# Which rows of the matrix form a block: blocks of neighbouring rows, or every 20th row (19th in the second half)

## The reference

```
a1 = adj * (y @ y.T);  a1 = a1 / max(rowsum(a1), 1e-12)
x  = layernorm(x + 0.9 * (a1 @ x) + 0.1 * h0)
f  = tanh(x @ W_proj + b_proj) @ W_gcn
x  = layernorm(x + relu(tanh(adj * adj) * (adj > 0) @ f + b_gcn))     # top 350 of a row; no row has more
```

## Time and profile before

| | |
|---|---|
| median of 3 runs | 485.69 us (484.28 to 486.65) |
| the profiled execution | 485.76 us, of which the span of the trace is 484.0 us |
| PE busy | 461.3 us, 95% |
| DVE busy | 378.4 us, 78% |
| ACT busy | 263.2 us, 54%, nearly all of it in the first 272 us |
| pass 1 ends, pass 2 begins | about 270 us |
| read from HBM, written | 105.57 MB, 2.56 MB |
| mean granted TensorE clock | 0.976 of full speed |

### The profile page before, as it was taken

One profiled execution on the slowest core, in us unless ns is written; L12 is line 12 of the kernel. 1 busy time (PEld: TensorE's weight loads), 2 busy tenths in 40 slices (PEclk: granted clock), 3 DMA queues, 4 the chain that ended last, 5 costly groups with the idle time before them and its releaser, 6 DMA issues.

```text
span 484.0 us, 15736 instructions
## 1 busy us (share of the span) xinstructions
PE 461.3 (95%) x5346; PEld 403.5 (83%) x5346; DVE 378.4 (78%) x1403; ACT 263.2 (54%) x357; POOL 160.0 (33%) x309
## 2 busy tenths in 40 slices
PE   6879999999999999999999999999999999999992
PEld 5767888888888888998888887888888888888881
DVE  4869999999989999999999966656656655655662
ACT  5877898899999999999999934600000000000000
POOL 3024433444445544444444431222122122112211
PEclk9688999999999999999999999999999999999997
DMA  8999999999999999999999100000000000000000
GB/s 236 366 394 420 400 377 389 348 371 395 394 419 414 416 419 418 420 419 419 419 420 422 57 1 1 13 17 11 16 16 11 16 16 16 11 16 16 11 16 15
DMA packets 33090, 108.56 MB, mean 224 GB/s; under 512 B 7801, under 2 KB 23058, under 8 KB 23058
## 3 DMA queue, kind: packets, MB, share of 16 engines
q1 hardware_dynamic: 33058, 108.14, 57.1%
HBM read 105.57 MB, written 2.56 MB: 223 GB/s over the span
## 4 chain that ended last, share of the span: by engine, by line
PE 72%; DVE 15%; issue 4%; DMA 3%; SPq 3%; ACT 1%; POOL 0%; DVEq 0%; POOLq 0%; ACTq 0%
PE acc L489 61%; PE words L476 5%; DVE a_bits L821 5%; DVE turned L808 3%; PE proj_acc L574 2%; SPq L320 2%; DMA a_rows<-in_adj_dram 2%; PE feat_acc L556 1%; DMA xs<-in_x_dram 1%; DVE z_high L864 1%; DVE z L871 1%; PE xnt_acc L548 1%; DVE stats L877 1%; DVE g_words L288 1%; DVE xn L826 1%
## 5 line engine op out<-in xcount | busy, mean ns | idle before, releaser
L489 PE MATMUL acc<-x_parts,turned 128*128 128x257 f16 (+1 forms) x1600 | 193.6, 274 | 0.3
L646 ACT ACTIVATE count_out<-a_rows,ones 128x2560 bf16<-128x2560 f32 (+1 forms) x80 | 189.9, 2373 | 0.4
L489 PEld LDWEIGHTS acc<-x_parts,turned 128*128 128x128 fp8e4 (+1 forms) x1600 | 155.1, 98 | 24.7 <-DVE x_parts L753 1.1
L489 PE MATMUL acc<-f_parts,turned 128*128 128x257 f16 (+1 forms) x1560 | 175.5, 273 | 0.0
L489 PEld LDWEIGHTS acc<-f_parts,turned 128*128 128x128 fp8e4 (+1 forms) x1560 | 151.3, 97 | 23.3 <-issue 0.4
L821 DVE TENSOR_SCALAR a_bits<-a_rows 128x2560 bf16<-128x2560 f32 (+1 forms) x80 | 116.6, 1458 | 9.9 <-DMA a_rows<-in_adj_dram 9.0
L808 DVE TENSOR_SCALAR turned<-a_words 128x320 uint16 (+1 forms) x305 | 66.7, 232 | 58.9 <-PE acc L489 58.8
L387 POOL TENSOR_TENSOR var_eps<-mean_var,consts 128x1 f32<-128x1 f32 x80 | 21.2, 266 | 231.8 <-DVE mean_var L1035 143.2
L390 POOL TENSOR_TENSOR rstd<-var_eps,consts 128x1 f32<-128x1 f32 x80 | 84.5, 1056 | 6.3
L808 DVE TENSOR_SCALAR turned<-same_class 128x320 uint16<-128x320 uint16 x313 | 63.7, 247 | 0.5
L476 PEld LDWEIGHTS words<-pack,a_bits 128*128 128x128 bf16 (+1 forms) x1600 | 53.3, 96 | 11.2 <-DVE a_bits L821 6.3
(11 more groups left out here) (112 smaller groups left out, 318.1 us busy)
## 6 DMA issues: line engine op xcount, KB each, us to landing
a_rows<-in_adj_dram SPq DMA_DIRECT2D x39, 1280.0 KB, 8.3
a_rows<-in_adj_dram SPq DMA_DIRECT2D x39, 1220.0 KB, 8.8
h_rows<-in_L_gnn_h_dram SPq DMA_DIRECT2D x39, 64.0 KB, 6.3
out_dram<-xn SPq DMA_DIRECT2D x39, 64.0 KB, 1.5
xs<-in_x_dram SPq DMA_DIRECT2D x3, 640.0 KB, 10.0
xs<-in_x_dram SPq DMA_DIRECT2D x1, 576.0 KB, 7.2
y_nat<-in_L_gnn_y_dram SPq DMA_DIRECT2D x1, 312.0 KB, 4.6
a_rows<-in_adj_dram SPq DMA_DIRECT2D x1, 80.0 KB
```

The lines of the kernel that those rows point to most:

```text
L489: mm = pe.matmul(acc[par][0:m, 0:PARTS], bits, parts[:, b, 0:PARTS], start=first and b == blocks[0], stop=last and b == blocks[-1])
L646: act.activation(count_out[0:m, 0:w], a_rows[par][h][0:m, 0:w], ACT.Relu, bias=ones[0:m, 0:1], scale=-HUGE, accum_out=col).then_inc(s_coun ...
```

## The change

Block b of the first half (b from 0 to 19) now holds rows 20p+b, p from 0 to 127 being the partition, and of the second half (b from 20 to 38) rows 2560+19p+(b−20). Block 39, the last 8 rows, is as before. For each partition the rows of all blocks of a half then lie next to each other in DRAM: one partition's `y` of a half is one run of 1280 or 1216 bytes where there were 64-byte rows, and a part of `x` is one run of 5120 or 4608 bytes where there were 512-byte rows. `y` comes in two DMAs (its semaphore counts to 32). The rows of `adj`, of `h0` and of the output are still one run per row and DMA (10,240 or 9760 bytes, and 512 bytes), but the 128 rows of a DMA lie 20 or 19 rows apart. The columns of `adj` that belong to column block b are every 20th (19th) too: packing takes as weights 128 bf16 bits with 20 or 19 elements between them in place of 128 neighbours. The loops that load and store are split at block 20, since the two halves have different strides.

```diff
-    def row_range(b, m):
-        return bass.ds(b * P, m)
+    RUN = [HB, FULL - HB]
+
+    def rows_in(a, b, half, m, cols):
+        if half is None:
+            return a[FULL * P:N, cols]
+        i = b - half * HB
+        v = a[half * HB * P:half * HB * P + RUN[half] * P, cols].rearrange("(p b) c -> p b c", b=RUN[half])
+        return v[:, i, :] if isinstance(i, int) else v[:, bass.ds(i, 1), :].rearrange("p a c -> p (a c)")
...
-        def block_view(a):
-            return a[0:FULL * P, :].rearrange("(b p) f -> p b f", p=P)
+        def blocks_in(a, part):
+            half = part.start // HB
+            v = a[half * HB * P:half * HB * P + RUN[half] * P, :].rearrange("(p b) f -> p b f", b=RUN[half])
+            return v[:, part.start - half * HB:part.stop - half * HB, :]
...
                 sp.dma_start(a_rows[par][h][0:m, 0:HALF[h].stop - HALF[h].start],
-                                 adj[row_range(t, m), HALF[h]]).then_inc(s_rows[par][h], 16)
+                                 rows_in(adj, t, half, m, HALF[h])).then_inc(s_rows[par][h], 16)
...
-            sp.dma_start(y_nat[:, 0:FULL, :], block_view(y)).then_inc(s_in["y"], 16)
+            for h, part in enumerate((slice(0, HB), slice(HB, FULL))):
+                sp.dma_start(y_nat[:, part, :], blocks_in(y, part)).then_inc(s_in["y"], 16)
...
                     k = rows_of(b)
-                    c = b * P - HALF[h].start
-                    mm = pe.matmul(words[par][0:k, b * WORDS:(b + 1) * WORDS],
-                                   a_bits[h][0:m, c:c + k], pack[0:m, :], start=True, stop=True)
+                    if b == LAST:
+                        bits = a_bits[h][0:m, RUN[h] * P:RUN[h] * P + k]
+                    else:
+                        bits = a_bits[h][0:m, 0:RUN[h] * P].rearrange("p (k b) -> p b k", b=RUN[h])[:, b - h * HB, :]
+                    mm = pe.matmul(words[par][0:k, b * WORDS:(b + 1) * WORDS], bits, pack[0:m, :],
+                                   start=True, stop=True)
```

More of the change, by code:

```diff
@@ L74, in at_cols, with half_of, in_halves @@
         return a[0:m, bass.ds(b, 1), lo:hi].rearrange("p a f -> p (a f)")
-    def row_range(b, m):
-        return bass.ds(b * P, m)
+    RUN = [HB, FULL - HB]
[5 more added lines that the diff above has]
+        return v[:, i, :] if isinstance(i, int) else v[:, bass.ds(i, 1), :].rearrange("p a c -> p (a c)")
+    def half_of(b):
+        return None if b == LAST else b // HB
+    def in_halves(eng, step, last):
+        for t in range(3):
+            step(t, t % 2, half_of(t))
+        for half, a, b in ((0, 3, HB - 1), (1, HB + 1, FULL)):
+            with eng.Fori((a - 1) // 2, (b - 1) // 2) as i:
+                step(i * 2 + 1, 1, half)
+                step(i * 2 + 2, 0, half)
+            if half == 0:
+                for t in range(b, HB + 1):
+                    step(t, t % 2, half_of(t))
+        for t in range(FULL, last):
+            step(t, t % 2, half_of(min(t, LAST)))
     def steps(eng, step, lag, after={}, first=3):
@@ L296, in _, with load_rows @@
         def _(sp):
-            def load_rows(t, par, pair):
+            def load_rows(t, par, half):
                 if not valid(t):
@@ L305, in load_rows, with load_h0 @@
                     sp.dma_start(a_rows[par][h][0:m, 0:HALF[h].stop - HALF[h].start],
-                                 adj[row_range(t, m), HALF[h]]).then_inc(s_rows[par][h], 16)
-            def load_h0(n, par):
+                                 rows_in(adj, t, half, m, HALF[h])).then_inc(s_rows[par][h], 16)
+            def load_h0(n, par, half):
                 m = rows_of(n)
@@ L311, in load_h0 @@
                     sp.wait_ge(s_xh, n - 1)
-                sp.dma_start(h0_rows[par][0:m, :], h0[row_range(n, m), :]).then_inc(s_h0[par], 16)
-            sp.dma_start(y_nat[:, 0:FULL, :], block_view(y)).then_inc(s_in["y"], 16)
+                sp.dma_start(h0_rows[par][0:m, :], rows_in(h0, n, half, m, slice(0, F))).then_inc(s_h0[par], 16)
+            for h, part in enumerate((slice(0, HB), slice(HB, FULL))):
+                sp.dma_start(y_nat[:, part, :], blocks_in(y, part)).then_inc(s_in["y"], 16)
             sp.wait_ge(s_cleared, 1)
@@ L318, in _ @@
             for q, part in enumerate(X_PART):
[L319 to L322, removed]
+                part = slice(part.start, min(part.stop, FULL))
+                sp.dma_start(xs[:, part, :], blocks_in(x, part)).then_inc(s_in[f"x{q}"], 16)
             sp.dma_start(xs[0:TAIL, FULL, :], x[FULL * P:N, :]).then_inc(s_in["xt"], 16)
             load_rows(1, 1, 0)
-            load_h0(0, 0)
-            load_h0(1, 1)
+            load_h0(0, 0, 0)
+            load_h0(1, 1, 0)
             sp.dma_start(wp[:, :], w_proj).then_inc(s_in["wp"], 16)
@@ L330, in _, with step, store @@
             sp.dma_start(bg_row[:, :], b_gcn.rearrange("(a p) -> a p", a=1)).then_inc(s_in["bg"], 16)
-            def step(t, par, pair):
+            def step(t, par, half):
                 if not isinstance(t, int) or t >= 2:
-                    load_rows(t, par, pair)
+                    load_rows(t, par, half)
                 if valid(t - 1) and (not isinstance(t, int) or t >= 3):
-                    load_h0(t - 1, (par + 1) % 2)
-            steps(sp, step, 4)
-            def store(t, par, pair):
+                    load_h0(t - 1, (par + 1) % 2, half_of(t - 1) if isinstance(t, int) else half)
+            in_halves(sp, step, NB + 1)
+            def store(t, par, half):
                 m = rows_of(t)
                 sp.wait_ge(s_result, t + 1)
-                sp.dma_start(out[row_range(t, m), :], xn[par][0:m, :]).then_inc(s_out[par], 16)
-            steps(sp, store, 0)
+                sp.dma_start(rows_in(out, t, half, m, slice(0, F)), xn[par][0:m, :]).then_inc(s_out[par], 16)
+            in_halves(sp, store, NB)
             sp.wait_ge(s_out[0], 16 * (NB // 2))
@@ L612, in _ @@
             act.wait_ge(s_cleared, 2)
-            act.wait_ge(s_in["y"], 16)
+            act.wait_ge(s_in["y"], 32)
             act.wait_ge(s_in["yt"], 16)
@@ L730, in _ @@
             dve.tensor_scalar(row_half[:, :], in_half[:, :], 0.0, None, ALU.is_gt).then_inc(s_packs, 1)
-            dve.wait_ge(s_in["y"], 16)
+            dve.wait_ge(s_in["y"], 32)
             dve.wait_ge(s_in["yt"], 16)
```

## The result

The changed kernel takes 529.9 us (529.19 to 530.85, 4 runs) against 486.17 us before (484.28 to 488.29): ratio 1.0896, 95% interval 1.0865 to 1.0928. The forecast was 483.5 us, with a range of 480 to 528. The changed kernel is 9% slower.

A forecast was written before the change was run, and what follows sets the result against it. The prediction took PE, without slack, to bound the steady steps, with the DMA next to its limit. From the profiled 485.76 us, −3.7 for the start and +1.4 for strided packing gave 483.5 us, range 480 to 528.

The forecast's parts named there:

- What bounds the kernel: Steady steps 17 to 39: PE has no slack, the DMA next to none; anything added to a packing pair is paid in full.
- The start: Kernel start: longer pieces of `y` and `x` let `adj` rows be issued earlier; −3.7 us, bounds 0 and −5.5.
- The second cast of block 1: Start, on DVE: its rows are there without the 2.19 us wait, so it comes 2.9 us earlier.
- the dummy products: Start, on PE: 40 products that took 3.81 us may run warm, up to 1.5 us gained, 0.8 taken.
- Block 0's cast: Start, on DVE: goes 0.67 us earlier, no more, since a memset at 9.37 stands ahead of it.
- Rows of `adj` apart, SP's loop, `h0` and the output: Loads, stores and SP's split loop: rows 20 apart and a few register instructions cost 0.
- Packing with strided weights: 1600 packing pairs on PE: between 0 and 2.7 us in all, middle +1.4 taken; bounds 0 and 299 us.
- The sign: Prediction wrong if a steady packing run is over 0.65 us, or block 1's second half is still waited for.
- A: Packing: a strided load needs twice its time and cannot use 2.4 GHz; 53 ns a pair, +45 us, 527 us; chance 0.13.
- B: Packing: the 128 columns are loaded one after another; 107 ns a pair, +131 us, 613 us; chance 0.14.
- C: Steady steps: scattered rows of `adj` are read more slowly, at 371 GB/s; +19 us, 501 us; chance 0.06.
- D: Start: its gain is lost to dummy products, clock and early steps, or new DMAs are no faster; 485.8 us; chance 0.07.

The follow-up runs named there:

- e3: The kernel before with only `y` and `x` loaded in long runs; 482.65 us, ratio 0.9912.
- e4: The kernel before with only packing's weights read 20 (19) columns apart, all loads as before; 533.31 us, ratio 1.0947.
- e1: The changed kernel with packing reading 128 neighbouring columns as weights again, its loads and row order kept; 483.83 us, ratio 0.9939.
- e7: The changed kernel with one packing pair behind each 257-column product from step 17 on, half 1 cast a little earlier; 518.89 us, ratio 1.0678.
- e5: The kernel before with packing of steps 3 to 16 reading bf16 weights at column steps from 1 to 20; 497.56 us (a single run).
- e10: The kernel before with packing of steps 3 to 16 reading fp8 weights at column steps of 1 to 38 bytes; median spacings 25 to 62 ns.
- e6: The kernel before with blocks in pairs: packing reads every 2nd column, `x` in 1024-byte and `y` in 128-byte pieces; 483.95 us, ratio 0.9955.
- e9: The changed kernel with packing pairs behind products from step 3 on, started later, the last block packed in one run; 494.4 us, ratio 1.018.

## Why the prediction was wrong

**What bounds the kernel.** Right, and it is what made the error dear: no slack on PE, so 35 ns a pair became 1.30 us a step.

**The start.** Right for the loads by themselves: −3.7 forecast, −3.9 measured (e3). The second cast of block 1 came 3.1 us earlier for 2.9 forecast, the dummy products gave 1.4 where 0.8 of 1.5 was taken. In the changed kernel the forecast did not hold at its place: the cast came 1.9 us earlier, the dummy products ran at clock 0.50, and step 3 begins only 0.3 us earlier. Of the 3.4 us by which the changed kernel is still under e4, 2.6 lie in steps 3 to 16, where e4 spent 6.8 us at half clock and the changed kernel none; no run tests whether the clock alone makes them. Block 0's cast, forecast 0.67 us earlier, came 0.9 us earlier in e3 (9.23 against 10.10) and 0.3 in the changed kernel (9.79), where the memset ahead of it on DVE came later (9.69 against 9.37). And the lower bound, −5.5, is more than the terms give, which is 2.9 + 1.5 = 4.4.

**Rows of `adj` apart, SP's loop, `h0` and the output.** The forecast was 0, and e1, which has all of them, shows the steady loop unchanged.

**Packing with strided weights: the step that failed.** The prediction took 27 ns for the load at half clock, so 13 at full clock, and put a strided read at half that rate, hidden but for 1.7 ns a pair: +1.4 us. Measured are 35 ns a pair and +46.8 us (e4). So it had 27 ns for a strided load at full clock, and measured are 60. The larger part of the miss is the clock: it was assumed that the strided read gets twice as fast with the array's clock, which it does not. The smaller part is the rate: against the packed load's 27 ns at half clock the strided one costs 2.2 times as much, not twice. In the changed kernel a run packed in a mostly cold stretch takes as long as a warm one, and so does the first run of e7, all of it at half clock:

```profile
26.20:27.50 1.30, 1.27 (x20) 1.28 (x20) 1.30 (x1) 0.00 (x0) 1.30 (x1) 1.00 0.96 366
27.80:29.20 1.40, 1.40 (x25) 1.35 (x23) 0.81 (x3) 0.00 (x0) 1.14 (x3) 0.61 1.07 449
11.10:12.40 1.30, 1.23 (x20) 1.26 (x20) 1.30 (x3) 0.48 (x2) 0.00 (x0) 0.50 0.98 406
```

Each window holds one run of 20 loads, 1.30, 1.30 and 1.31 us long, at a mean clock of 1.00, 0.61 and 0.50, and the median spacing is 60, 59 and 60 ns. The row of 27 ns at half clock told how the packed load goes with the clock, and nothing of a strided read. With bounds of 0 and 299 us and no row for such a read, a cost of 1.4 us was a choice and no estimate. The upper bound was not in the same measure either: its 212 ns are the duration of one load, and 25 ns is a spacing.

**The sign.** A packing run over 0.65 us in the steady loop was to show the prediction wrong. The kernel before has 0.66 and 0.74 there, since the first load of a run lies under the product ahead of it. The spacing inside the run, 25 against 60 ns, tells the two apart.

**The rivals.** A had the right place, the right sign and nearly the right total: 527 us against 529.9. Part of that is luck. Its 53 ns a pair were 7 too few, which makes +45 us if all 1600 pairs pay in full; measured are 60 ns, which would be +56, but only 46.8 came, since the steps before 17 did not pay in full. Its argument, a read that cannot use the array's clock, is what the windows above show; that the cost is one of 16-byte lines is what e5 and e10 show. It had a chance of 0.13. The range ended at its round number, 528, with no room for A's own uncertainty, although all between A and B was open. B (107 ns), C and D did not come, D in so far as the start's gain is there in e3.

**The rules drawn on.** Of the Trainium skill, the rule of SBUF — State Buffer, section "Door 1: The DMA port swizzle", that lines of 16 bytes set the cost of a stride, is borne out by e5 and e10. Its limits are not: it has a bf16 stride free up to 8 elements and two hits a line enough, while here step 4 (two elements a line) costs 34 ns and step 8 the full 60. The rule of the same skill that spoke for the change, TensorE: Matmul & The Clock Gate, section "Weight-path perf modes", that the fast load takes strided columns, says nothing of their time. The runs show loads of 128 columns at every column step tried, 60 ns apart at steps 19 and 20; whether they are still made in the fast way no run here tells.

## What to carry to other kernels

- A strided weight load of 128 columns is priced by the 16-byte lines that its columns touch. Here a pair took about 0.5 ns a line, but never less than 25 ns: column steps of up to 6 bytes were free, 16 bytes and more cost 60 ns. A layout that made the DMA pieces longer by a factor of 2 instead of 20 had 2.5 of the 3.9 us of gain without the price (e6).
- On an engine without slack, an access pattern that no row shows is the term to settle first. If it cannot be settled, the forecast belongs nearer to the middle of what is open, and the range has to end beyond the likely rival.
- Where a slow load is needed, put it behind a long product: at 128 rows it was hidden in full (e7), though the best such version (e9) stayed 10 us behind the one that avoids the slow load (e6). The 8-row loads between products on 128 rows were not hidden.

## What was not expected of the hardware

- The strided load's 60 ns do not depend on the granted clock (1.00, 0.61 or 0.50), while the packed load's spacing goes from 25 to 27 ns.
- An 8-row load and product between 128-row products made the group last 374 ns instead of 135, both at clock 1.00 (486 ns at 0.50).
- Going from 64-byte and 512-byte to 1280-byte and 5120-byte pieces raised the first slice from 236 to 308 GB/s (e3), and SP was held by the four parts of `x` for 2.50 us instead of 10.72.
